# Projections of a two-layer attention block: three fp16 products of split X and split weights, in chunk order

## The reference

```python
qkv = jnp.einsum('oc,bchw->bohw', w_qkv, x)          # 768 x 256 weights, 256 x 4096 tokens
q, k, v = jnp.split(qkv, 3, axis=1)                  # 8 heads of 32 channels each
scores = jnp.einsum('bhdi,bhdj->bhij', q, k) / sqrt(32)
out = jnp.einsum('bhij,bhdj->bhdi', softmax(scores), v)
x = jnp.einsum('oc,bchw->bohw', w_proj, out) + x     # layer 0
# layer 1: 1x1 convolutions g, theta, phi, 2x2 max pooling, a second softmax attention
# over 4096 x 1024, a 1x1 convolution W with batch norm, and + x
```

## Time and profile before

| | |
|---|---|
| median of 3 runs | 2709.13 us (2707.6 to 2714.66) |
| the profiled execution | 2712.51 us, span 2710.8 us |
| PE busy | 2553.2 us (94% of the span) |
| ACT busy | 2223.1 us (82%) |
| DVE busy | 2162.7 us (80%) |
| mean granted TensorE clock | 0.983 |
| Q and K projections on PE (L253) | 128.1 us in 256 records |
| V projections on PE (L267) | 59.5 us in 512 records |

### The profile page before, as it was taken

One profiled execution on the slowest core, in us unless ns is written; L12 is line 12 of the kernel. 1 busy time (PEld: TensorE's weight loads), 2 busy tenths in 40 slices (PEclk: granted clock), 3 DMA queues, 4 the chain that ended last, 5 costly groups with the idle time before them and its releaser, 6 DMA issues. The chain is left out here.

```text
span 2710.8 us, 58233 instructions
## 1 busy us (share of the span) xinstructions
PE 2553.2 (94%) x24658; PEld 747.2 (28%) x24666; DVE 2162.7 (80%) x1414; ACT 2223.1 (82%) x2490; POOL 403.5 (15%) x588
## 2 busy tenths in 40 slices
PE   7999999989999999698979999999899999995999
PEld 4222222242222222243442222222422222222434
DVE  3889999948899999586538999999489999994864
ACT  4999999949999999237439999999499999991474
POOL 0111111101111111011001111111011111110100
PEclk9999999999999999899989999999999999998999
DMA  2556666605566566201115665665056656652011
GB/s 83 110 126 126 126 125 127 126 17 110 126 124 127 121 127 126 86 11 48 41 69 117 126 128 121 127 126 121 16 121 124 128 121 127 127 121 79 11 51 43
DMA packets 89277, 272.03 MB, mean 100 GB/s; under 512 B 17504, under 2 KB 18592, under 8 KB 88608
## 3 DMA queue, kind: packets, MB, share of 16 engines
q0 software_dynamic: 64512, 234.91, 42.7%
q1 hardware_dynamic: 24480, 33.16, 3.6%
HBM read 22.88 MB, written 8.68 MB: 12 GB/s over the span
## 5 line engine op out<-in xcount | busy, mean ns | idle before, releaser
L490 DVE TENSOR_TENSOR acc<-acc,P 128x2048 f32<-128x2048 f32 x704 | 1613.4, 2292 | 83.2 <-ACT P L459 15.3
L459 ACT ACTIVATE P<-scores 128x1536 f32<-128x1536 f32 x1024 | 1594.8, 1557 | 0.0
L381 PE MATMUL psOL<-P,V 128*32 128x512 f32 (+1 forms) x8960 | 1074.3, 567 | 1.4 <-ACT P L459 1.4
L372 PE MATMUL psOL<-Q,K 32*128 32x512 f16 x3072 | 842.7, 380 | 28.0 <-ACT P L458 17.3
L372 PE MATMUL scores<-Q,K 32*128 32x512 f16 x9216 | 849.2, 380 | 0.0
L458 ACT ACTIVATE P<-psOL 128x512 f32<-128x512 f32 x1024 | 711.9, 695 | 36.9 <-PE scores L372 36.9
L515 POOL DMA_DIRECT2D accD<-P x384 | 335.7, 998 | 1231.9 <-ACT P L459 1022.4
L372 PEld LDWEIGHTS psOL<-Q,K 32*128 32x128 f16 x3072 | 207.5, 93 | 986.0 <-ACT P L458 855.7
L381 PEld LDWEIGHTS psOL<-P,V 128*32 128x32 f32 x8960 | 196.9, 108 | 474.4 <-issue 438.5
L372 PEld LDWEIGHTS scores<-Q,K 32*128 32x128 f16 x9216 | 220.8, 93 | 0.0
L253 PE MATMUL scores<-X,wq_sb 128*128 128x512 f32 x256 | 128.1, 631 | 40.5 <-DMA X<-in_x 28.1
(11 more groups left out here) (113 smaller groups left out, 1499.3 us busy)
## 6 DMA issues: line engine op xcount, KB each, us to landing
accD<-P POOLq DMA_DIRECT2D x448, 512.0 KB, 5.2
X<-in_x SPq DMA_DIRECT2D x16, 512.0 KB, 7.1
R<-att_inv SPq DMA_DIRECT2D x32, 256.0 KB
out<-res SPq DMA_DIRECT2D x32, 256.0 KB, 2.0
R<-pool_inv SPq DMA_DIRECT2D x2, 2048.0 KB, 7.1
TB<-TA SPq DMA_DIRECT2D x2, 512.0 KB, 4.6
wq_sb<-in_w_qkv SPq DMA_DIRECT2D x1, 768.0 KB, 4.4
Ls<-L SPq DMA_DIRECT2D x32, 8.0 KB
```

What stands on the lines that cost most here:

```text
L372: last = nc.tensor.matmul(dst[h], K[rows, kp, j * 128:(j + 1) * 128], Q[rows, qp, cs], start=(n == 0), stop=(n == 2))
L381: last = nc.tensor.matmul(both[h * D:(h + 1) * D, lo:hi], V[:, j, h * D:(h + 1) * D], P[:, r + h, lo:hi], start=(j == 0), stop=(j == JT - 1))
L459: nc.scalar.activation(P[:, r + 1:r + G, :], bank[n % 2].rearrange("p (u n) -> p u n", n=CH), ACT.Exp, scale=SCORE).then_inc(s_exp, 1)
L490: nc.vector.tensor_tensor(acc[:], old, P[:, r:r + G, :], ALU.add).then_inc(s_add, 1)
```

## The change

The stage is rewritten in four respects.

1. X and the projection weights are split into fp16 high and low parts. `wq_hi` and `wq_lo` are made once, in the setup block, by one ACT and one DVE instruction of 128x1536. `Xh` (ACT, `high`) and `Xl` (DVE, `low`) are made chunk by chunk, 128x1024 each, in each of the four stages. A projection is then three fp16 products: high weight by Xh, low weight by Xh, high weight by Xl. The fp32 weights stay in a tile of the setup block.
2. The work goes chunk by chunk: Q unit, K unit and value unit of chunk c, then chunk c + 1. A Q or K unit is 6 fp16 matmuls of 512 columns, a value unit 24 of 128 columns. The six banks hold two chunks.
3. The order on the engines: ACT makes Xh of chunk c + 1 before it serves chunk c, DVE makes Xl of chunk c + 1 likewise. `norms` of chunk c - 1 stand behind the units of chunk c, and the last two `norms` behind the last value unit. The transpose for the bound is the last instruction of PE.
4. ACT copies V for all eight value units, DVE for none.

The diff, cut to its core (lines that rename tiles, declare semaphores or clear them are left out):

```diff
-wq_sb = sb(root, "wq_sb", [128, CT, 3 * C])
+wq = [sb(root, f"wq_{n}", [128, CT, 3 * C], F16) for n in ("hi", "lo")]
...
+        dve.wait_ge(s_wq, 1)
+        nc.vector.scalar_tensor_tensor(out=wq[1][:], in0=wq32[:], scalar=WS, in1=wq[0][:],
+                       op0=ALU.mult, op1=ALU.subtract).then_inc(s_wq, 1)
+        dve.wait_ge(s_wq, 2)
...
+        nc.scalar.activation(wq[0][:], wq32[:], ACT.Copy, scale=WS).then_inc(s_wq, 1)
...
+    def unit(c, k):
+        w = 3 * c + k
+        if w >= 6:
+            pe.wait_ge(s_ve if k == 2 else s_ev, c - 1 if k == 2 else 2 * (c - 2) + k + 1)
+        outs = slice(k * C + g * 128, k * C + (g + 1) * 128)
+        for n, (wp, xp) in enumerate(((0, Xh), (1, Xh), (0, Xl))):
+            if n == 0:
+                pe.wait_ge(s_xh, c + 1)
+            if n == 2:
+                pe.wait_ge(s_xl, c + 1)
+            for t in range(CT):
+                last = nc.tensor.matmul(slot(w), wq[wp][:, t, outs],
+                                        xp[:, t, c * CH:(c + 1) * CH],
+                                        start=(n == 0 and t == 0), stop=(n == 2 and t == CT - 1))
         last.then_inc(s_mm, 1)
...
+    def value_unit(c):
+        if c >= 2:
+            pe.wait_ge(s_ve, c - 1)
         for r in range(4):
...
+            js = slice((4 * c + r) * 128, (4 * c + r + 1) * 128)
             for t in range(CT):
...
+                for n, (xp, wp) in enumerate(((Xh, 0), (Xh, 1), (Xl, 0))):
+                    last = nc.tensor.matmul(
+                        slot(3 * c + 2)[:, r * 128:(r + 1) * 128], xp[:, t, js],
+                        wq[wp][:, t, 2 * C + g * 128:2 * C + (g + 1) * 128],
+                        start=(t == 0 and n == 0), stop=(t == CT - 1 and n == 2))
         last.then_inc(s_vm, 1)
...
+    for c in range(NC):
+        unit(c, 0)
+        if c:
+            norms(2 * c - 2)
+        unit(c, 1)
+        if c:
+            norms(2 * c - 1)
+        value_unit(c)
+    norms(NU - 2)
+    norms(NU - 1)
+    pe.wait_ge(s_b, 2)
+    nc.tensor.transpose(psO[0:1, 0:128], bound[:, 2:3], ident[:, :]).then_inc(s_nm, 1)
...
+    def high(c):
         cs = slice(c * CH, (c + 1) * CH)
...
+        if g == 0:
+            act.wait_ge(s_x[c], 16)
+        nc.scalar.activation(Xh[:, :, cs], X[:, :, cs], ACT.Copy, scale=QS).then_inc(s_xh, 1)
+    high(0)
+    for c in range(NC):
+        cs = slice(c * CH, (c + 1) * CH)
+        if c + 1 < NC:
+            high(c + 1)
+        for k in range(2):
+            u = 2 * c + k
+            act.wait_ge(s_mm, u + 1)
+            nc.scalar.activation(QK[k][:, 0, cs], slot(3 * c + k), ACT.Copy, scale=1.0 / WS
+                                 ).then_inc(s_hi, 1)
+            if u >= 2:
+                act.wait_ge(s_nm, u - 1)
+            act.wait_ge(s_hi, u + 1)
+            nc.scalar.activation(sq[u % 2][:], QK[k][:, 0, cs], ACT.Square).then_inc(s_sq, 1)
+        act.wait_ge(s_vm, c + 1)
+        nc.scalar.activation(V[:, 4 * c:4 * c + 4, :].rearrange("p j n -> p (j n)"), slot(3 * c + 2),
+                             ACT.Copy, scale=1.0 / (QS * WS)).then_inc(s_ve, 1)
...
+    def low(c):
         cs = slice(c * CH, (c + 1) * CH)
...
+        dve.wait_ge(s_xh, c + 1)
+        nc.vector.scalar_tensor_tensor(out=Xl[:, :, cs], in0=X[:, :, cs], scalar=QS,
+                                       in1=Xh[:, :, cs], op0=ALU.mult, op1=ALU.subtract
+                                       ).then_inc(s_xl, 1)
+    low(0)
+    for c in range(NC):
+        cs = slice(c * CH, (c + 1) * CH)
+        if c + 1 < NC:
+            low(c + 1)
+        for k in range(2):
+            u = 2 * c + k
+            dve.wait_ge(s_hi, u + 1)
+            nc.vector.scalar_tensor_tensor(
+                out=QK[k][:, 1, cs], in0=slot(3 * c + k), scalar=1.0 / WS, in1=QK[k][:, 0, cs],
+                op0=ALU.mult, op1=ALU.subtract).then_inc(s_ev, 1)
+            if u >= 2:
+                largest(u - 2)
```

More of the change, by code:

```diff
@@ L145, in conv_seq @@
             s_hd = sem(ctx, "s_hd")
-            loads = [(wq_sb[:], wqkv.rearrange("(t p) o -> p t o", p=128)),
+            loads = [(wq32[:], wqkv.rearrange("(t p) o -> p t o", p=128)),
                      (wp_sb[:], wproj.rearrange("(t p) o -> p t o", p=128)),
@@ L223, in layer0 @@
                         sq = [sb(c2, f"sq{k}", [128, CH], BF16) for k in range(2)]
+                        Xh = sb(c2, "Xh", [128, CT, N], F16)
+                        Xl = sb(c2, "Xl", [128, CT, N], F16)
                         nmax = sb(c2, "nmax", [128, 2 * NC])
+                        s_xh = sem(c2, "s_xh")
+                        s_xl = sem(c2, "s_xl")
                         bound = sb(c2, "bound", [128, 4])
@@ L243, in norms @@
                                                      ).then_inc(s_nm, 1)
[L245 to L254, removed]
-                                    last.then_inc(s_mm, 1)
-                                    if u >= 2:
-                                        norms(u - 2)
@@ L271, in _ @@
-                                    last.then_inc(s_vm, 1)
-                                    if q < 2:
-                                        norms(NU - 2 + q)
-                                    if q == 3:
-                                        pe.wait_ge(s_b, 2)
-                                        nc.tensor.transpose(psO[0:1, 0:128], bound[:, 2:3], ident[:, :]).then_inc(s_nm, 1)
+                                            for n, (xp, wp) in enumerate(((Xh, 0), (Xh, 1), (Xl, 0))):
[3 more added lines that the diff above has]
+                                                    start=(t == 0 and n == 0), stop=(t == CT - 1 and n == 2))
@@ L289, in _ @@
-                                for q in range(1, JT // 4, 2):
-                                    act.wait_ge(s_vm, q + 1)
-                                    act.wait_ge(s_ve, q)
-                                    nc.scalar.copy(V[:, 4 * q:4 * q + 4, :].rearrange("p j n -> p (j n)"), slot(NU + q)
-                                                   ).then_inc(s_ve, 1)
+                                    if g == 0:
+                                        act.wait_ge(s_x[c], 16)
+                                    nc.scalar.activation(Xh[:, :, cs], X[:, :, cs], ACT.Copy, scale=QS).then_inc(s_xh, 1)
@@ L323, in _ @@
                                                         ).then_inc(s_b, 1)
-                                for q in range(0, JT // 4, 2):
-                                    dve.wait_ge(s_vm, q + 1)
-                                    if q:
-                                        dve.wait_ge(s_ve, q)
-                                    nc.vector.tensor_copy(V[:, 4 * q:4 * q + 4, :].rearrange("p j n -> p (j n)"), slot(NU + q)
-                                                          ).then_inc(s_ve, 1)
                                 dve.wait_ge(s_b, 4)
@@ L341, in _ @@
                                     sp.wait_ge(s_st, 16)
-                        end_phase(c2, s_x + [s_mm, s_ev, s_hi, s_st, s_sq, s_nm, s_nx, s_vm, s_ve, s_b])
+                        end_phase(c2, s_x + [s_xh, s_xl, s_mm, s_ev, s_hi, s_st, s_sq, s_nm, s_nx, s_vm, s_ve, s_b])
                     with ExitStack() as c2:
```

32 lines of the change are left out of this document (4 added, 28 removed).

## The result

The changed kernel takes 2691.2 us (median; 2690.43 to 2692.71), the one before, in the same comparison, 2711.89 us (2707.6 to 2714.97). The ratio is 0.9925, with a 95% interval of 0.9912 to 0.9938. The forecast difference was -26.1 us, the measured one is -20.7 us on the medians and -22.1 us between the two profiled spans.

What follows compares the result with a forecast made beforehand. PE alone was taken to bound the projection stages; -41.2 (PE) + 7.5 (ends) + 2.2 (starts) + 2.4 (setup) + 3 (clock) = -26.1 us, giving a median of 2683.0 us, range 2671 to 2702.

Steps and rivals of the forecast that it cites:

- PE's work: Projection stages: fp16 products cut PE's work from 45.18 to 34.87 us per stage, 41.24 us less in four stages.
- the ends' 7.5: End of each projection stage: last norms, reductions and bound chain no longer covered, +1.9 us per stage, +7.5 in all.
- halving the fp32 spacing: Value units: fp16 matmuls of 128 columns taken at 111.7 / 2 = 55.9 ns spacing, gaining 3.56 us per stage.
- Rivals 2 and 3: Value units: weight loads hide only partly, +16 us, chance 0.10; or spacing set per load-matmul pair, +43 us, chance 0.06.
- The 81 ns: Value units: the skill's rule for a load and matmul pair at 128 columns, which would cost 19.3 us more.
- ACT and DVE: Mid-stage: ACT needs 3.84 us and DVE 3.6 us per chunk, both under PE's 4.36, so their new work costs nothing.
- The starts: Start of stages: Xh of chunk 0 ahead of the first matmul, +1.1 us in first and third stage, +2.2 in all.
- I take 0, since the head start is longer than both: Second and fourth stage's start: Xh and Xl ready when PE comes, 3.16 us after SP, so no cost.
- the 2.2 kept for the range: Second and fourth stage's start: if ACT and DVE arrive with PE, 1.1 us each, counted only in the range.
- The setup's +2.4: Setup block: two 128x1536 split instructions ahead of the old split delay the first stage by 2.4 us, once.
- The clock in attention: Attention stages: PE's longer idle ahead of them may bring low clock, +3 us taken, bounds -6.8 to +10.
- half of the way to the first stage's price: Attention stages: the +3 us clock term, between no falls and all four falling as the first did, +6.4 us.

Runs made afterwards that it cites:

- x6: Changed kernel with value units by fp32 matmuls from X, only Q and K by fp16 products: 2710.21 us.
- x3: Changed kernel without the third product (high weights by Xl) in all projections, Xl still made: 2676.67 us.
- x4: Changed kernel with all V copies on DVE instead of ACT, behind a chunk's two reductions: 2695.24 us.
- x9: Kernel before with the last two norms and the transpose behind the last value unit, ACT copying all V: 2727.45 us, ratio 1.0055 to before.
- x1: Changed kernel with chunk 6's value unit behind chunk 7's units and the last one behind the last norms: 2683.03 us, ratio 0.9889 to before.
- x2: Changed kernel plus unread fp16 matmuls at each stage's end, five behind the last norms, four behind the transpose: 2683.48 us, ratio 0.989 to before.

## Why the prediction was right, and where its terms were off

**PE's work: right.** -10.31 us per stage rested on 0.2155 us and 55.9 ns. The spacing is 56 ns, the chunk 4.36 us. With the ends' 7.5 the four stages were to be 33.7 us shorter, and they are 33.8. That it is so close is in part luck: the single stages were to be 8.4 us shorter each and are 7.4, 9.0, 9.5 and 8.0. The slow start of each stage was left as it was in the sum; its length changed by +2.0, -1.1, -2.2 and +0.7 us, half of which is lost or won, and over four stages that nearly cancels. For the same reason the first stage takes 42.4 us from its first Xh (18.75), where 41.3 were expected. The step for which no row existed, halving the fp32 spacing, gives the right number; that the loads hide is shown (98 ns each at 56 ns spacing), the reason given, that the fp16 load is half as long, was not tested. Rivals 2 and 3 are refuted by the same rows, and x6 shows the value units' 0.445 us per chunk. The 81 ns of the Trainium skill (TensorE: Matmul & The Clock Gate, section Back-to-back issue gap) do not hold for this stream: the trace has 56.

**ACT and DVE: right.** 3.84 us for ACT was worked out from overlaps of other instructions, and x3 measured 3.84; the parts are each off by some hundredths (4.06 us recorded instead of 4.10, overlaps of 0.40 instead of 0.44), which cancel. x4 shows that DVE has room for the V copies too.

**The ends: right in size.** From the last `norms` (57.48, whose columns end 0.22 later) to attention are 3.4 us, where 3.6 was expected, and 0.33 of waiting for DVE ahead of it, which the text did not name. Together that is 3.8. x9 gives 2.0 us per stage for the same edit by itself.

**The starts: too low by 2.1 us.** The sum had 2.2 for X's two stages and 2.4 for the setup, 4.6; measured are 3.7, 0.5, 2.2 and 0.3, in all 6.7. The step that failed is "I take 0, since the head start is longer than both": ACT does not arrive when SP does but 2.6 us after it (552.26 and 554.83), so PE waits 0.5 and 0.3 us in the second and fourth stage; that lies within the 2.2 kept for the range. In the first, X's transfer took 0.2 us longer. In the third, 0.7 us were lost between the end of attention and SP's start, which is layer 1, and 0.3 in the transfer. In layer 1 the profile of the change has a stretch at the low clock that the one before has not (windows 150 us into layer 1, before and then the change):

```profile
1247.00:1252.00 5.00, 2.13 (x10) 0.77 (x10) 3.18 (x2) 4.94 (x5) 0.00 (x0) 1.00 0.62 227
...
1236.00:1241.00 5.00, 3.90 (x12) 1.49 (x13) 3.66 (x3) 4.94 (x5) 0.00 (x0) 0.66 0.86 360
```

In all, the clock is low there for 31.4 us instead of 25.8. That may be the 0.7 us; no run shows it. The setup's +2.4 is right: SP starts at 14.74 instead of 12.35.

**The clock in attention: the mechanism right, the size too low by 2.0 us.** I took +3, measured are +5.0. The step that failed is "half of the way to the first stage's price": the prediction took the bare end to raise a chance, and it brought the fall in all 20 stages that have one. The price per fall was read well from before (3.3), and it is 2.9 here (488.7 against 485.7 for a stage without it). How much that is against the kernel before depends on its execution: those that ran beside x1 to x9 took 2707.6 to 2721.7 us, at a mean granted clock of 0.986 to 0.978.

The span difference came out 4.0 us above the forecast (-22.1 for -26.1) through these two terms. The median came out 8.2 us above it (2691.2 for 2683.0), within the range given. The other 4.2 us are no term of the sum: 2.8 are the median of the kernel before, 2711.89 in this comparison and 2709.13 in the runs that the forecast started from, and 1.4 are the difference between profiled executions and medians (-22.1 against -20.7).

## What to carry to other kernels

An fp32 matmul that is replaced by three fp16 products costs three quarters of the time, if the parts are made by engines with idle time; order the work so that this making is spread over all of the matrix engine's work, not only over the part that needs it first. When work is regrouped, look at what the last piece used to cover: here moving two value units towards the end, the last of them behind the last `norms`, gave back 4.7 us in the projections and, through the clock, as much again in attention, of which 6.9 us remained in the whole span. An idle matrix engine just ahead of a sparse stage had a price in that next stage here, which no row of the changed stage shows.

## What the runs showed of the hardware

- fp16 matmuls of 128 columns, each with a full 128x128 weight load of its own, start 55.8 ns apart over runs of 24, that is 28 ns per instruction, loads counted (changed kernel). The loads are recorded at 98 ns and hide entirely.
- With the bare end PE does nearly nothing for 3.4 us and then waits for ACT; the granted clock then fell to 0.50, the 1.2 GHz level, in all 20 such stages of five kernels. In the changed kernel it fell 0.1 to 1.3 us after attention's first matmul and came back 13.7 us later. Extra matmuls at such a place (x2) made attention 5.6 us shorter in sum.
- An attention stage's length goes with how long its clock is low: 485.6 to 486.0 us with no fall, 486.9 with 3.4 us of it, 487.2 to 488.2 with 6.8, 488.5 or more with 13.7 or more.
- A projection stage begins with matmuls at half the later rate for 2.7 to 5.9 us, in the second stage of the kernel before at a granted clock of 0.51 (559.4 to 565.4). The stages' lengths of two kernels differ by half the difference of this time (x4's first stage against the changed kernel's: 2.1 us less of it).
- ACT instructions that wait for nothing start up to 0.11 us before the recorded end of the one ahead, in this mix too (33.22 + 1.05 against 34.16, and 36.58 + 0.58 against 37.06).
